# Ending the four blocks of an embedding, state-space and expert kernel without GpSimd's drain

## Time and profile before

| | us |
|---|---|
| median of three runs | 1768.21 |
| lowest, highest | 1763.48, 1771.48 |
| the profiled execution | 1780.81 |
| its span, first to last instruction | 1779.1 |
| PE busy in the span | 1574.6 |
| POOL busy in the span | 781.5 |

### The profile page before, as it was taken

The page is one execution under the profiler, slowest core; times in us unless marked ns, Lnnn a source line. Parts: engine busy times, 40 slices in busy tenths (PEclk is TensorE's granted clock), DMA queues, the critical chain, the costliest instruction groups (busy, mean ns, idle before and its releaser), DMA issues. The chain is left out here.

```text
span 1779.1 us, 31373 instructions
## 1 busy us (share of the span) xinstructions
PE 1574.6 (89%) x9263; PEld 1146.1 (64%) x9264; DVE 971.2 (55%) x2325; ACT 730.3 (41%) x1592; POOL 781.5 (44%) x638
## 2 busy tenths in 40 slices
PE   7999999997599999999999670099999999999996
PEld 7999999975477576675766340066655666666564
DVE  5555554523768998889789545034333343433443
ACT  2525253522776765857658100033333333333332
POOL 4230300011042357677675567545544555555554
PEclk9999999988799998998899575599999999999999
DMA  7210000003355352443423110167767777777665
GB/s 267 77 60 1 13 1 13 1 18 134 114 152 143 93 153 77 134 130 93 151 64 90 27 37 2 60 181 190 159 154 188 162 181 167 169 183 182 162 114 92
DMA packets 97703, 195.20 MB, mean 110 GB/s; under 512 B 38391, under 2 KB 46879, under 8 KB 92880
## 3 DMA queue, kind: packets, MB, share of 16 engines
q0 software_dynamic: 36992, 88.26, 23.1%
q1 hardware_dynamic: 60624, 105.78, 19.5%
HBM read 144.15 MB, written 49.84 MB: 109 GB/s over the span
## 5 line engine op out<-in xcount | busy, mean ns | idle before, releaser
L1888 PE MATMUL moe_ps_gu<-moe_wgu,moe_xt 128*128 x960 | 331.9, 489 | 0.0
L1746 POOL DMA_INDIRECT out_h<-moe_yy,moe_idx_s x121 | 190.9, 1578 | 256.2 <-DVE moe_idx_s L1808 117.4
L1016 POOL DMA_INDIRECT scratch_slots<-lay_toki,lay_slot x192 | 219.9, 1145 | 59.0 <-issue 58.1
L1888 PEld LDWEIGHTS moe_ps_gu<-moe_wgu,moe_xt 128*128 128x128 f32 x960 | 173.7, 191 | 96.6 <-issue 1.2
L1785 ACT ACTIVATE moe_sl<-moe_ps_gu 128x192 f32<-128x192 f32 x120 | 39.7, 331 | 365.7 <-PE moe_ps_gu L1888 336.2
L1411 DVE SCALAR_TENSOR_TENSOR lay_xa<-lay_ring,head_cw,lay_xa 128x378 f32<-128x378 f32 (+5 forms) x240 | 141.9, 609 | 54.4 <-ACT lay_xa L1068 46.0
L1197 PE MATMUL lay_ring<-lay_xnt,win_sb 128*128 128x128 f32 (+2 forms) x1152 | 167.6, 292 | 4.3 <-DVE lay_xa L1411 2.0
L1281 PE MATMUL lay_ring<-head_wout,lay_yb 128*128 128x512 f32 x384 | 170.1, 597 | 0.0
L1197 PEld LDWEIGHTS lay_ring<-lay_xnt,win_sb 128*128 128x128 f32 (+2 forms) x1152 | 150.6, 200 | 10.5 <-issue 3.8
L1740 POOL DMA_INDIRECT moe_xg<-scratch_xg,moe_idx_g x123 | 131.4, 1069 | 47.5 <-issue 28.7
L247 POOL TENSOR_TENSOR tok_vv<-tok_w 128x512 f32<-128x512 f32 x16 | 16.6, 1040 | 259.7 <-ACT tok_w L449 225.5
(11 more groups left out here) (290 smaller groups left out, 2961.5 us busy)
## 6 DMA issues: line engine op xcount, KB each, us to landing
lay_m<-scratch_cum SPq DMA_DIRECT2D x16, 1536.0 KB
moe_wgu<-in_wgu SPq DMA_DIRECT2D x32, 768.0 KB
moe_wd<-in_wd SPq DMA_DIRECT2D x32, 384.0 KB
out_h<-lay_hres SPq DMA_DIRECT2D x48, 128.0 KB
scratch_xg<-lay_x SPq DMA_DIRECT2D x48, 128.0 KB
win_sb<-in_win SPq DMA_DIRECT2D x1, 4384.0 KB, 16.3
tok_u_raw<-in_tok_u SPq DMA_DIRECT2D x16, 256.0 KB, 4.5
tok_v_raw<-in_tok_v SPq DMA_DIRECT2D x16, 256.0 KB, 5.1
```

The source lines that it names most:

```text
L1016: pool.indirect_dma_start(out=a["slots"], out_offset=bass.IndirectOffsetOnAxis(ap=slot[:, j, k:k + 1], axis=0), in_=toki[:, j:j + 1], in_o ...
L1746: pool.indirect_dma_start(out=a["out"], out_offset=bass.IndirectOffsetOnAxis(ap=idx_s[n][:, 0:1], axis=0), in_=yy[n][:], in_offset=None, b ...
L1888: last = mm(ps_gu[b][:], xt[b][:, t], wgu[:, bass.ds(r * KD + t, 1)].rearrange("p o n -> p (o n)"), start=t == 0, stop=t == KD - 1)
```

## The change

Each of the four `nc.Block()` gets `no_gpsimd_drain=True`. ACT, PE, DVE and SP are then ended with a plain drain each, GpSimd with none, and behind them stands a barrier over all five engines that is made of event instructions on semaphores only: the four others raise the gather semaphore with an event instruction of their own, and GpSimd waits for it and releases them. The barrier ahead of block 1 is not changed, and no instruction inside a block is.

```diff
@@ -173,7 +173,7 @@
-        with nc.Block() as block:
+        with nc.Block(no_gpsimd_drain=True) as block:
```

## The result

| | before | after |
|---|---|---|
| median of 18 runs each, us | 1770.57 | 1760.21 |
| lowest, highest | 1762.40, 1776.42 | 1751.70, 1768.78 |
| profiled execution, its span | 1780.81, 1779.1 | 1759.92, 1758.2 |

The ratio is 0.9941, with a 95% interval of 0.9922 to 0.9959: 0.59% faster, 10.4 us of 1770.6, with 7.3 to 13.8 us in the interval. The forecast was 10.26 us less and a median of 1758 us, from 1752 to 1768; measured were 1760.21 us, against a kernel before whose median of 18 runs is 2.4 us above that of the three runs the forecast started from.

A forecast was written before the change was run, and what follows sets the result against it. No engine was taken as full (PE busy 89%); what counted was who comes last at the four barriers. From a median of 1768.21 us, minus 7.90 minus 2.51 plus 0.15 gave 1757.95, say 1758 us, range 1752 to 1768.

The forecast's parts named there:

- The drain behind block 3, minus 7.90: Barrier behind block 3: GpSimd's 7.897 us drain is alone on the path, so all of block 4 moves up 7.90 us.
- The drain behind block 4, minus 2.51: End of the span: GpSimd's 2.508 us drain has nothing of the kernel after it, so 2.51 us are saved.
- Blocks 1 and 2 and the added events: Barriers behind blocks 1 and 2: drains hidden by SP's stores, removal worth 0; added events cost 0.1 to 0.2 us.
- plus 0.15: Cost taken for the added event instructions, on the path only behind blocks 1 and 2, where SP is last.
- The sum: Minus 7.90 minus 2.51 plus 0.15 is minus 10.26 us for the whole kernel.
- The reason that was given against deferral: Block 4's 121 scatters and 123 gathers keep a flat length with no drain between them, for 600 us.
- The deferral rival: First gather of block 4 meets block 3's queue, takes 1.07 plus 7.9 us; time 1765.9 or 1768.4 us; chance 0.14.
- The slower rival: Block 4 starts with a full queue and each GpSimd DMA pays, 0.2 us more per scatter: 1782 us; chance 0.06.

The follow-up runs named there:

- the fifth block: Changed kernel plus a block of GpSimd alone behind block 4: batches of gathers and scatters, a drain behind each; long batches' drains 7.147, 4.407, 1.181 us, no kernel time given.

## Why the prediction was right

**The drain behind block 3, minus 7.90.** Right in place and size. GpSimd was last by 14 us, nothing moved up into the hole, and block 4 started as a whole: from GpSimd's branch to the release it is 0.3 us, where it was 8.2. Taken alone it measured 7.1 (2.5 to 11.7) us.

**The drain behind block 4, minus 2.51.** Right by the trace: the span ends 0.4 us behind the branch, and the 1.7 us around it stayed. By time alone it is within its interval, 3.4 (-1.4 to 8.2). The rule of the Trainium skill that was weighed here, from "VectorE: DVE Perf Modes", "The DRAIN you can't avoid", would still leave drains behind the kernel; no run shows any, and if one is there it does not pay for the queue within the measured time.

**Blocks 1 and 2 and the added events.** Worth nothing within the interval, as forecast. The plus 0.15 is too small for any of the times; in the traces SP's drain and its release behind blocks 1 and 2 start 0.2 and 0.1 us apart before, and 0.2 and 0.2 after.

**The sum.** The two drains are read directly, 7.9 and 2.5 us. That the medians differ by 10.4 us, within 0.1 of the forecast, is luck: the interval is 7.3 to 13.8 us.

**The reason that was given against deferral was half right.** I argued from the flat length of 244 DMA instructions that a full queue does not trouble its users. Retirement does happen in the users' stream. It does not lengthen the instruction, it stands as idle time "issue" ahead of it, and I had not looked there. It is cheap: 0.6 us in block 3 of both kernels, 0.8 and 0.6 us at the 14th and 18th DMA of block 4 where block 3's drain is left out, 1.1 to 2.7 us in the fifth block for up to 113 entries, where a drain would take 9.3 us for them (113 x 82 ns, beyond the 82 DMAs to which the line was measured). The deferral rival was to show 7.9 us at the first gather of block 4 and showed 0 there; what comes later is at most 1.5 us and goes into waits that GpSimd has anyway. So of this rival the mechanism was there and the price was not. (The prediction counts 3 DMAs ahead of block 4's first scatter; it is 4, and nothing hangs on it.)

**A step that was open.** I noted that 224 DMAs cost 7.9 us and 244 only 2.5, and drew nothing from it. The queue is emptied in bulk on the way, and a drain pays only for what is left. How much that is, is settled for none but the fifth block, and there only by the reading of two sets: block 3's 96 of 224 and block 4's 30 of 244 stay open.

**The slower rival** needed scatters of 1.74 us or more; they stayed at 1.58.

No version beyond the changed kernel followed from the experiments: of the kernels with a drain left in that were measured in several runs, none gained more than 0.40%.

## What to carry to other kernels

Look at the closing barrier's line for the drain of the engine that issues software DMAs, and at who comes last: here a drain of GpSimd cost 82 ns for each DMA left in its queue although all had landed, and it is on the path wherever GpSimd closes the block. This program waits for every one of those DMAs by semaphore before the barrier; only under that condition was leaving the drain out tried. To see whether the work comes back later, compare the idle time ahead of each DMA, and not only the length of the instructions. For effects of this size read the changed instructions themselves, and leave the difference of two spans alone.

## What the runs showed of the hardware

- A GpSimd drain takes 0.03 to 0.05 us plus 82 ns for each of its DMAs since the queue was last emptied, up to 82 of them (0, 24, 28, 42, 70, 72, 82 DMAs: 0.046, 1.997, 2.324, 3.482, 5.774, 5.922, 6.744 us). In every one of these cases all DMAs had landed; no run shows a drain with a DMA still on its way. Gathers of whole rows, scatters of whole rows with an add and scatters of 4 bytes count the same.
- The 114th such DMA after a drain, or after the start, starts 0.6 to 2.7 us late, for gathers, scatters and a mix; all of these move 128 rows. Behind it a drain is shorter than the number of DMAs would make it (200 gathers: 7.147 us; 200 scatters with an add: 4.407 us; 244 in turn: 1.181 us).
- In one trace the 61st, 121st and 181st scatter with an add after a drain start 0.76 us late too, and in a mix of them with gathers the 79th, 157th and 235th DMA 0.9 us.
- A queue that is not drained behind block 3 costs GpSimd 0.7 to 0.8 us ahead of the 14th and 0.6 us ahead of the 18th DMA of block 4, in four traces of four; five traces with the drain have neither.
- A second drain right behind the first takes 0.046 us.
